# Own order per engine, float32 probabilities for half the heads, maxima in halves

## The reference, cut to what matters

```python
x = x + _L0_cond_ref(x, itok_B_0_7, weight, bias)              # x1
x = x + _L1_cond_ref(x, zX, zY, zR, 1, 1)                      # x2
score_prev = einsum('bhqd,bhkd->bhqk', q, k_prev) * SCALE      # masked by length
score = concatenate([score_prev, (q * k_self).sum(-1) * SCALE], -1)
weights = softmax(score)                                       # 16 heads, 256 x 257
x = x + (weights_prev @ v_prev + weights_self * v_self) @ Wo + bo   # x3
s0, s1, eo = (relu(x @ wi_e) @ wo_e for e in (shared 0, shared 1, chosen))
w = softmax(relu(concatenate([eo[:, 0], s0[:, 0], s1[:, 0]]) @ g1) @ g2)
x = x + eo * w[0] + s0 * w[1] + s1 * w[2]
```

## Time and profile before

| | |
|---|---|
| median of 3 runs | 1146.88 us (1146.86 to 1148.57) |
| profiled execution, its own time | 1148.39 us |
| its span, first to last instruction | 1146.8 us |
| granted PE clock, mean over the span | 0.967 of full speed |
| busy: PE, DVE, ACT, POOL | 988.7, 868.9, 603.8, 568.5 us |
| one turn of the loop, `self` to `self` | 66.7 us (569.62 to 636.29) |

### The profile page before, as it was taken

The page is one execution under the profiler, slowest core; times in us unless marked ns, Lnnn a source line. Parts: engine busy times, 40 slices in busy tenths (PEclk is TensorE's granted clock), DMA queues, the critical chain, the costliest instruction groups (busy, mean ns, idle before and its releaser), DMA issues.

```text
span 1146.8 us, 27267 instructions
## 1 busy us (share of the span) xinstructions
PE 988.7 (86%) x9456; PEld 922.6 (80%) x9456; DVE 868.9 (76%) x1710; ACT 603.8 (53%) x1177; POOL 568.5 (50%) x432
## 2 busy tenths in 40 slices
PE   4558988998898999889899888989898898989886
PEld 4228888888888888888888888888888888888785
DVE  3576787877778787777878777787877778787733
ACT  3354654646565464656546455655645565554532
POOL 6573636455463645446364544636454463644422
PEclk9559999999999999999999999999999999999988
DMA  4725233251524324152422415242241524223110
GB/s 133 161 74 84 76 70 65 69 92 37 92 74 72 74 61 88 37 92 74 76 80 55 83 37 92 74 80 86 48 80 37 92 74 83 83 55 73 39 46 10
DMA packets 79339, 83.46 MB, mean 73 GB/s; under 512 B 11444, under 2 KB 74708, under 8 KB 79316
## 3 DMA queue, kind: packets, MB, share of 16 engines
q1 hardware_dynamic: 79316, 83.15, 32.0%
...
## 4 chain that ended last, share of the span: by engine, by line
PE 38%; DVE 30%; issue 12%; DMA 10%; ACT 6%; SPq 2%; POOL 1%; DVEq 1%; ACTq 0%; POOLq 0%
DMA k_rows<-prob_lo 7%; PE front L586 4%; DVE prob_hi L950 4%; PE out L488 4%; PE out L489 4%; PE out L490 4%; PE hid L488 4%; PE hid L490 4%; PE hid L489 4%; PE front L597 3%; DVE s_max L930 3%; DMA q_rows<-max_rows 3%; DVE hid_lo L1004 2%; PE front L488 2%; SPq L421 2%
## 5 line engine op out<-in xcount | busy, mean ns | idle before, releaser
L821 ACT ACTIVATE hid_hi<-hid 128x512 fp32r<-128x512 f32 x192 | 114.6, 597 | 251.5 <-PE hid L490 250.8
L488 PE MATMUL out<-hid_hi,exp_hi 128*128 128x256 f32 x768 | 230.1, 300 | 14.7 <-DVE hid_lo L1004 14.6
L1136 POOL TENSOR_TENSOR prob_lo<-prob,prob_hi 128x512 f16<-128x512 f32 x128 | 162.9, 1273 | 137.3 <-ACT prob_hi L781 137.3
L488 PE MATMUL hid<-x_hi,exp_hi 128*128 128x256 f32 x768 | 226.7, 295 | 2.2 <-DVE x_lo L1000 2.2
L930 DVE TENSOR_REDUCE s_max<-front 128x2 f32<-128x512 f32 x256 | 165.2, 688 | 77.0 <-PE front L586 76.0
L489 PE MATMUL out<-hid_lo,exp_hi 128*128 128x256 f32 x768 | 216.8, 282 | 0.0
L490 PE MATMUL out<-hid_hi,exp_lo 128*128 128x256 f32 x768 | 216.5, 282 | 0.0
L489 PE MATMUL hid<-x_lo,exp_hi 128*128 128x256 f32 x768 | 214.5, 279 | 0.0
L490 PE MATMUL hid<-x_hi,exp_lo 128*128 128x256 f32 x768 | 214.4, 279 | 0.0
L1086 POOL TENSOR_TENSOR exp_lo<-raw,exp_hi 128x512 fp32r<-128x512 f32 (+1 forms) x80 | 154.8, 1946 | 104.5 <-ACT exp_hi L794 104.3
L777 ACT ACTIVATE prob<-front 128x512 f32<-128x512 f32 x256 | 146.8, 600 | 63.4 <-PE front L597 61.7
...
## 6 DMA issues: line engine op xcount, KB each, us to landing
...
q_rows<-prob_hi SPq DMA_DIRECT2D x96, 128.0 KB, 4.2
k_rows<-prob_lo SPq DMA_DIRECT2D x96, 128.0 KB, 4.6
...
```

The lines of the kernel that those rows point to most:

```text
L488: nc.tensor.matmul(acc, w_hi, a_hi, start=first, stop=False)
L821: nc.scalar.activation(hid_hi[:, s % 2, :], hid_bank[s % 2][:, :], ACT.Relu).then_inc(hid_hi_done, 1)
L1136: nc.gpsimd.tensor_tensor(prob_lo[:, h % NPROB, :], prob[:, h % NPROB, :], prob_hi[:, h % NPROB, :], ALU.subtract).then_inc(prob_split_poo ...
```

## The change

1. **Own order per engine.** `BODY` is replaced by five lists. The ring of PSUM banks follows PE's list, and each kind of use has semaphores of its own.

```diff
-STEP = [("S7", "H4 x_parts"), ("S8", "w_parts"), ("S9", "P3"), ("S10", "s_parts"), ("S11", "H5 wo_part0"),
...
+PE_BODY = """
+H0 S0 S1 H1 S2 S3 P0 S4 S5 H2 S6 S7 P1 H3 m0 S8 S9 P2 H4 S10 S11 P3
+E0 H5 E1 S12 P4 E2 S13 H6 E3 S14 P5 E4 S15 H7 E5 P6 E6 m1 H8 E7
+x1 P7 q E8 H9 E9 lap P8 E10 E11 H10 E12 kp P9 E13 H11 E14 P10 E15 P11 pvend
+ks gate aT vs logits wo vp self logits_free
+""".split()
+ACT_BODY = """
+H0 wi0 H1 wi1 H2 wi2 wi3 x_parts H3 m0 H4 w_parts P3 E0 H5 E1 E2 H6 wo0 E3 E4 wo1 H7 E5 s_parts E6 m1 H8 wo2 E7
+x1_parts wo3 react P7 q E8 H9 E9 qa x2_parts E10 E11 qb H10 E12 kp E13 kq H11 E14 E15 P11 ks aT vs logits x3_parts vp sum
+""".split()
+DVE_BODY = """
+S0 S1 H0 S2 S3 H1 S4 S5 S6 H2 S7 H3 S8 S9 x_parts S10 H4 S11 S12 E1 H5 S13 H6 S14 E3 S15 H7 E5 H8 E7
+x1 x1_parts react H9 lap half x2_parts H10 kp k3 H11 att relu aT logits mix scale wo x3_parts vp self
+""".split()
+POOL_BODY = """
+wi0 wi1 wi2 wi3 x_parts w_parts E0 E2 wo0 E4 wo1 s_parts E6 m1 wo2 wo3 x1 qa norm qb ks sum vp
+""".split()
+SP_BODY = """
+m0 wo_load m1 x1 lap wi_load qb E15 kp k3 sum
+""".split()
```

```diff
                     for k in range(C):
-                        at = k * S + t * P
-                        nc.tensor.matmul(acc, prob_hi[:, h % NPROB, at:at + P], v_cols[:, k, h, :], start=(k == 0), stop=False)
...
+                        at, start, stop = k * S + t * P, k == 0, k == C - 1
+                        if h < HALF:
...
+                        else:
+                            acc = pv[:, t, (h - HALF) * VF:(h - HALF + 1) * VF]
+                            last = nc.tensor.matmul(acc, prob[:, h % NPROB, at:at + P], v_full[:, k, h - HALF, :], start=start, stop=stop)
```

```diff
-                    for c in range(C):
-                        last = nc.tensor.matmul(out_bank[c][:, S:S + 1], gate_terms[:, c * P:(c + 1) * P], ones[:, :], start=True, stop=True)
+                    wait(pe, e_out_done, NE, j, NE)
+                    for c in range(C):
+                        for e in range(NE):
+                            for k in range(C):
+                                last = nc.tensor.matmul(out_bank[c][:, S:S + 1], gate1[:, (e + 1) % NE * C + k, c * P:(c + 1) * P],
+                                                        e_out[:, e, k, 0:1], start=((e, k) == (0, 0)), stop=((e, k) == (NE - 1, C - 1)))
```

```diff
+                    half = int(name[1])
+                    wait(pe, max_split, 2, i, half + 1)
                     for t in range(C):
-                        last = nc.tensor.transpose(psum[0:H, t * P:(t + 1) * P], s_max[:, t, :], ident[:, :])
+                        last = nc.tensor.transpose(psum[0:3 * HALF, :].bitcast(BF16)[:, t * P:(t + 1) * P],
+                                                   m_parts[:, t, half, :], ident_half[:, :])
```

```diff
+                elif name == "E15":
+                    wait_filled(sp, i, name)
+                elif name == "kp":
                     sp.dma_start(k_rows[MASK_ROW:MASK_ROW + 1, :, :],
                                  mask_dram[bass.ds(i, 1), :].unsqueeze(1).to_broadcast([1, H, S])).then_inc(mask_placed, 16)
...
                     place(q_rows, Q_BANDS, q_parts, 0, q_placed)
...
                     place(q_rows, Q_BANDS, q_parts, 1, q_placed)
...
                     place(q_rows, Q_BANDS, q_parts, 2, q_placed)
-                elif name == "kp":
-                    wait(sp, k_part_done, 2 * C, i, C)
+                    wait(sp, k_part_done, 2 * C, i, 2 * C)
                     place(k_rows, K_BANDS, k_parts, 0, k_placed)
-                    wait(sp, k_part_done, 2 * C, i, 2 * C)
                     place(k_rows, K_BANDS, k_parts, 1, k_placed)
-                    wait_freed_dve(sp, i, "kp")
+                elif name == "k3":
+                    wait(sp, k_split, 1, i, 1)
                     place(k_rows, K_BANDS, k_parts, 2, k_placed)
```

More of the change, by code:

```diff
@@ L81 @@
-FIRST_HALF = ATTENTION.index("S5") + 1
-DVE_LATER = {"H2": "S1", "H3": "S5", "H4": "S9", "H5": "S13", "H6": "mT", "aT": "relu"}
-AFTER = {name: rest.split() for name, rest in STEP}
-FRONT = ATTENTION[FIRST_HALF:] + EARLY + ATTENTION[:FIRST_HALF]
-BODY = [x for stage in FRONT for x in [stage] + AFTER.get(stage, [])]
-DVE_BODY = list(BODY)
-for name, later in DVE_LATER.items():
-    DVE_BODY.remove(name)
-    DVE_BODY.insert(DVE_BODY.index(later) + 1, name)
-LAGS = (EARLY + ATTENTION[:FIRST_HALF] + ["x_parts", "w_parts", "s_parts", "x1_parts", "x2_parts", "react", "self"],
-        ATTENTION[FIRST_HALF:] + ["half", "norm", "pvend", "att", "aT", "wo", "x3_parts"]
-        + [x for stage in ATTENTION[:FIRST_HALF] for x in AFTER.get(stage, []) if x not in ("sum", "self", "store")])
@@ new lines, with lag @@
+m0 wo_load m1 x1 lap wi_load qb E15 kp k3 sum
+""".split()
+S_OF, E_OF = [f"S{h}" for h in range(H)], [f"E{h}" for h in range(H)]
+PRESENT = "x_parts w_parts s_parts x1 x1_parts react q qa qb lap x2_parts ks vs kp kq k3 vp self".split()
+PREVIOUS = S_OF + E_OF + "m0 m1 half norm pvend att aT wo x3_parts wi_load".split()
+def lag(name):
+    return 0 if name in PRESENT else 1 if name in PREVIOUS else 2
+FAMILIES = {"S": H, "E": H, "m": 2, "x1": 1, "q": 1, "lap": 1, "ks": 1, "vs": 1, "kp": 1, "vp": 1, "self": 1}
@@ L97, with family @@
+ACT_FREES = ("E", "m", "q", "ks", "vs")
+def family(name):
+    if name in FAMILIES:
+        return name, 0
+    return (name[0], int(name[1:])) if name[0] in FAMILIES and name[1:].isdigit() else (None, 0)
+RING = [x for x in PE_BODY if family(x)[0]]
+assert len(RING) % 2 == 0 and len(RING) == sum(FAMILIES.values())
+EARLY = ("x_parts", "x1", "react", "lap")
+SHARED_AT = ["ks", "vp", "E0", "E2", "E4", "E6", "m1", "E8"]
+SHARED_POOL = SHARED_AT[:-1] + ["norm"]
 SHARED = len(SHARED_AT)
+SP_FIRST = "m0 wo_load E0 E2 E4 E6 m1 x1 lap wi_load qb E15 kp k3 vp sum".split()
@@ L115 @@
-N_LO_POOL = [h + 1 - N_LO_DVE[h] for h in range(H)]
+BEHIND = 2
+N_LO_DVE = [sum(g % 2 for g in range(h + 1)) for h in range(HALF)]
+N_LO_POOL = [h + 1 - N_LO_DVE[h] for h in range(HALF)]
 BQ, BK, BO, BV, B_PREV, B_SELF, NVEC = range(7)
-LINKS = {"early": 4, "attention": 4 + H // 2, "rest": NE * C + 2}
+LINKS = {"early": 4, "attention": 8, "rest": 3}
 def wait(eng, sem, per_turn, turn, n):
@@ L182, in build @@
         v_rest = beside
+        k_rest = beside
+        q_rest = s_raw
         q_full = sb("q_full", [P, C, S])
@@ L542, in attend @@
                 last.then_inc(pv_done, 1)
             def front(name, i):
-                if name == "self":
-                    wait(pe, qk_done, 1, i, 1)
-                    for t in range(C):
-                        for c in range(C):
-                            last = nc.tensor.matmul(pv_bank[0][:, t * H:(t + 1) * H], ksT[:, c, t * P:(t + 1) * P],
-                                                    head_ones[:, c * H:(c + 1) * H], start=(c == 0), stop=(c == C - 1))
-                    last.then_inc(self_done, 1)
-                    return
@@ L578, in front @@
                     last = token_major(psum, linear(2), x_hi, x_lo)
+                elif name == "self":
+                    wait(pe, qk_done, 1, i, 1)
+                    for t in range(C):
+                        for c in range(C):
+                            last = nc.tensor.matmul(psum[:, t * H:(t + 1) * H], ksT[:, c, t * P:(t + 1) * P],
+                                                    head_ones[:, c * H:(c + 1) * H], start=(c == 0), stop=(c == C - 1))
                 elif name[0] == "S":
@@ new lines, in front @@
+                        by_head = att[:, t, HALF * DH:D].rearrange("p (h d) -> p h d", d=DH)
+                        linkf(nc.vector.tensor_tensor(by_head, sums[:, t, :, 0:DH], own, ALU.add))
+                    for t in range(C):
+                        by_head = att[:, t, HALF * DH:D].rearrange("p (h d) -> p h d", d=DH)
+                        last = nc.vector.tensor_tensor(by_head, by_head, den[:, t, heads].unsqueeze(2).to_broadcast([P, HALF, DH]), ALU.mult)
+                    last.then_inc(att_done, 1)
```

468 lines of the change are left out of this document (242 added, 226 removed), and 5 rows, old and new, of the table STEP.

## The result

The changed kernel takes **1320.3 us** (median of 4 runs, 1318.9 to 1324.3), the kernel before 1146.9 beside it: a ratio of 1.152, with a 95% interval of 1.149 to 1.155. I had predicted slower, but by 4% and not by 15%: 1194, with 1230 as the upper end.

A forecast was written before the change was run, and what follows sets the result against it. PE was taken as the bound: 67.1 us of work plus 2.7 of waits make a turn of 69.8, +3.1. 1146.8 + 1.4 + 14 x 3.1 + 2.2 = 1193.8 of span, so 1194 us; range 1152 to 1230.

The forecast's parts named there:

- The float32 heads, +4.8 us: PE, heads 8 to 15: each head's products take 0.80 us instead of 0.20, adding 4.8 us a turn.
- the rival of float32 at float16's price: PE's float32 products cost what float16 ones do: turn 62.9 us, 1097 us in all; chance 0.06.
- The gate, +2.2 us: PE: twelve one-column gate products, 24 records, take 2.7 us instead of 0.47, adding 2.2 us a turn.
- PE's work, 67.1 us: PE's busy time per turn after the change: 60.1 + 4.8 + 2.2 us.
- "What is late next", 2.7 us: Waits left along PE's new list, 2.7 us a turn together, where 6.6 us of idle time stood.
- E9's wait for `q_full`: PE, ahead of one score step, waits 0.4 us a turn for ACT's `q_full`.
- head 8's for `half`: PE, ahead of head 8's products, waits 0.9 us a turn for `half`, behind a chain of DVE operations.
- S9 waits for ACT's copy of `m0`, 0.7: A PE step sharing the bank of `m0` waits 0.7 us for six short DVE operations and then ACT.
- The clock at 1.00 in the loop: Granted PE clock, 1.00 in the present turn; the forecast counted no loss for it in its 14 turns.
- Placements just covered, 0: Twelve transfers of q and k land at 16.3 us, when PE reaches the step needing them; no wait counted.
- Outside the loop: Stretches before and after the 14 turns: +1.4 us for the first turns, +2.2 us for the end.
- "The orders block one another": Rival: five in-order engine lists wait for each other, idle time stays 6.6 us, turn 73.7, 1248 us; chance 0.10.

The follow-up runs named there:

- m0_cover: Changed kernel with only one hidden-layer step on PE moved ahead of the `m0` transposes, to cover DVE's six small operations; 1284.3 us, ratio 1.122.
- best_pegate: Changed kernel reordered to cover all three PE waits, with GpSimd kept clear of DVE's small operations; float32 heads and gate on PE kept; 1190.0 us, ratio 1.038.
- pool_away: Changed kernel with ACT's and GpSimd's work on the first chosen matrix's last quarter and x's parts moved behind `m0`; 1264.3 us, ratio 1.103.
- filled_waits2: Changed kernel with dummy products put into PE's three long waits, which themselves stay in place; 1284.6 us, ratio 1.121.
- f32_wide: Changed kernel with float32 products of heads 8 to 15 widened from 17 to 49 columns, all else kept; 1325.6 us, ratio 1.154.
- before_f32_heads: Kernel before with only heads 8 to 15 changed to float32 probabilities and one product; orders, gate and maxima as before; 1202.1 us, ratio 1.047.
- best_f32: `best_pegate` with the gate's sum back on DVE as in the kernel before, and one PE step moved to cover it; 1183.5 us, ratio 1.032.
- front_order: Changed kernel with four operations moved on ACT, DVE and GpSimd, aimed at the waits for `q_full` and `half`; 1295.6 us, ratio 1.129.

## Why the prediction was wrong

A turn of 78.5 us is now: 67.1 of work, 5.1 of waits, and 6.3 that are left for the clock (13.6 us at half clock; 5.6 to 6.1 by the two turns of `m0_cover`). I had 67.1 + 2.7 + 0.

- **The float32 heads, +4.8 us: right.** 0.81 us a head as against 0.80. The row that I chose (the head sum, same type and weights) was the right one; the rival of float32 at float16's price is refuted here, and the table of the Trainium skill (TensorE: Matmul & The Clock Gate, Back-to-back issue gap), about 60 cycles for 1 to 64 moving columns with no word of the type, does not give the price of these products. The same section says that the table is for an isolated product and that in a stream with a weight load for each product both set the spacing; the rows here fit that (17 and 49 columns take the same time, and the loads last 191 ns for float32 and 97 for float16), though no run shows that the loads set the spacing.
- **The gate, +2.2 us: right** (2.60 against my 2.7). In the old orders the two parts came out cheaper, 2.5 and 0.4 us a turn, because each takes operations from other engines for which PE had waited; the prediction counted 0.3 us of such waits for the gate, and PE's idle time fell by 1.5.
- **PE's work, 67.1 us: right**, 67.0 by `best_pegate`.
- **"What is late next", 2.7 us: the first step that failed.** It measured 5.1. E9's wait for `q_full` was 1.0 where I had 0.4, head 8's for `half` 1.6 where I had 0.9, H0's 0.4 where I had 0.5. The error of size is largest at "S9 waits for ACT's copy of `m0`, 0.7": the wait stands one step earlier, at `m0` itself, and is 2.1 us. I had priced six short operations as short. Two of them take 1.2 us each behind GpSimd, and `pool_away` showed that this makes the wait: the two took 2.05 us less, and the 2.1 us went. GpSimd stands in the other two chains as well, as the trace of the changed kernel shows; no run took this apart from the orders:

```profile
603.70 0.69 DVE L1006 SCALAR_TENSOR_TENSOR prob_lo<-prob,prob_hi 128x512 f16<-128x512 f32 x1 [0.36 <-ACT prob_hi L841]
...
616.85 1.53 DVE L1006 SCALAR_TENSOR_TENSOR prob_lo<-prob,prob_hi 128x512 f16<-128x512 f32 x1 [0.80 <-ACT prob_hi L841]
...
616.54 1.29 POOL L1132 TENSOR_TENSOR exp_lo<-raw,exp_hi 128x512 fp32r<-128x512 f32 x1
...
623.42 0.75 DVE L952 SCALAR_TENSOR_TENSOR react<-beside,z_sb,react 128x512 f32<-128x512 f32 x1 [1.16 <-POOL beside L1147]
```

  In E9's chain the split of head 7 takes 1.53 us beside GpSimd and 0.69 without it, 0.8 more ahead of `x1`. In head 8's chain my list left out DVE's sum L952, 0.75 us, which waits for GpSimd's `beside` and stands ahead of the rest of H9.
- **The clock at 1.00 in the loop: the step that I never took.** The sum multiplies a turn "at a granted clock of 1.00" by 14. In the kernel before it was 1.00 with 6.6 us of idle time, but in pieces of 1.1 us at most; the change leaves less idle time, in pieces of 2.1 and, close together, 1.0 and 1.6. `m0_cover`, `pool_away` and `filled_waits2` show that each fall behind `m0` goes with the idle time; behind head 8 filling the waits took away 6.8 of 10.2 us in the mean. 6.3 us x 14 = 88 us of the 129 by which the span of 1322.4 lies above my 1193.8; the waits give 34 and the stretches outside the loop 7.
- **Placements just covered, 0: right** in the loop. No steady turn waits for `k_rows`.
- **Outside the loop:** +6.4 and +4.2 where I had +1.4 and +2.2, 7 us in all.
- **The rivals.** "The orders block one another" (0.10) was nearest, with 1248; it had the kind of loss right, but its idle time of 6.6 us was above what came, and its time 72 us below, since it too had no clock in it.

What stays open: why the fall behind head 8 lasts 10.2 us with float32 heads and 3.4 with float16 ones. It is not the columns (`f32_wide`), and how it divides between the waits and the float32 products is not shown: without a wait ahead of them the float32 heads brought 3.4 us in every second turn of the old orders (`before_f32_heads`), none in `best_f32`, and 0, 3.4 or 6.8 us in the steady turns of `filled_waits2`. And the fall comes in some turns and not in others with the same waits (`m0_cover`, `front_order`, where the wait of 2.1 us at `m0` was followed by a fall in 7 of 14 turns). I can't say from these runs which turn will have one. The start was not taken apart.
